# Two groups of heads in one PSUM bank in both attentions of a six-layer decoder kernel on one Trainium2 core

## What is computed

```python
for i in range(NL):
    xn = _adaln(x, noise_emb, n1_w[i], n1_b[i])
    qkv = xn @ qkv_w[i].T
    q, k, v = jnp.split(qkv, 3, axis=-1)
    q = _rope(q.reshape(B, L, H, HD))
    k = _rope(k.reshape(B, L, H, HD))
    v = v.reshape(B, L, H, HD)
    a = _attn(q, k, v, src_mask).reshape(B, L, D) @ so_w[i].T
    x = x + a
    xn = _adaln(x, noise_emb, n2_w[i], n2_b[i])
    q = _rope((xn @ cq_w[i].T).reshape(B, L, H, HD))
    k = _rope((context @ ck_w[i].T).reshape(B, LC, H, HD))
    v = (context @ cv_w[i].T).reshape(B, LC, H, HD)
    a = _attn(q, k, v, ctx_mask).reshape(B, L, D) @ co_w[i].T
    x = x + a
    xn = _adaln(x, noise_emb, n3_w[i], n3_b[i])
    h = jax.nn.gelu(xn @ f1_w[i].T + f1_b[i], approximate=False)
    x = x + (h @ f2_w[i].T + f2_b[i])
```

## Time and profile before

| | us |
|---|---|
| median of 3 runs | 2669.58 (2665.58 to 2670.88) |
| the profiled execution | 2669.4 |
| its span | 2667.6 |
| PE busy in the span | 2461.6 (92%) |
| DVE busy | 2051.6 (77%) |
| ACT busy | 1842.0 (69%) |
| POOL busy | 1079.4 (40%) |

### The profile page before, as it was taken

How to read it: one execution, slowest core, us unless ns; L and a number is a source line. 1 busy time by engine, 2 the same in 40 slices (tenths; PEclk the granted TensorE clock), 3 DMA queues, 4 the chain that set the end, 5 groups by cost and what they waited for, 6 DMA issues and landing times.

```text
span 2667.6 us, 45155 instructions
## 1 busy us (share of the span) xinstructions
PE 2461.6 (92%) x16138; PEld 1064.4 (40%) x16138; DVE 2051.6 (77%) x4303; ACT 1842.0 (69%) x3703; POOL 1079.4 (40%) x1342
## 2 busy tenths in 40 slices
PE   6999899999878899999999999999999999998777
PEld 3445454454512233333333333333333333333444
DVE  6778869778687788888888888888888888875333
ACT  4667666667326677887778877777887777878432
POOL 2545545545533333444344444333443334432311
PEclk9999999999869999999999999999999999999768
DMA  2000000000321121222222222212121212220000
GB/s 75 1 1 1 1 1 1 1 27 1 82 49 42 48 62 48 62 56 73 56 57 64 56 73 59 60 48 71 54 63 50 63 48 56 55 68 22 20 10 8
DMA packets 108569, 113.01 MB, mean 42 GB/s; under 512 B 15809, under 2 KB 96951, under 8 KB 107319
## 3 DMA queue, kind: packets, MB, share of 16 engines
q1 hardware_dynamic: 108345, 110.12, 15.1%
HBM read 14.80 MB, written 1.05 MB: 6 GB/s over the span
## 4 chain that ended last, share of the span: by engine, by line
PE 58%; DVE 22%; POOL 7%; issue 4%; DMA 3%; SPq 3%; ACT 3%; DVEq 0%; POOLq 0%; ACTq 0%
PE psum L1121 8%; DVE A L1591 7%; PE psum L1104 6%; PE psum L917 5%; PE psum L1092 4%; DVE A L1613 4%; PE psum L1027 4%; PE psum L1213 4%; PE psum L1220 3%; PE psum L1002 3%; PE psum L993 3%; SPq L814 2%; DVE nm L1461 2%; PE psum L1185 2%; DMA A<-A 2%
## 5 line engine op out<-in xcount | busy, mean ns | idle before, releaser
L1591 DVE TENSOR_REDUCE A<-psum 128x1 f32<-128x512 f32 x1536 | 1005.4, 684 | 191.8 <-PE psum L1104 178.1
L1808 ACT ACTIVATE A<-psum 128x512 f32<-128x512 f32 x1536 | 821.6, 602 | 149.0 <-PE psum L1121 78.9
L1104 PE MATMUL psum<-A 64*128 64x512 bf16 x1536 | 475.8, 391 | 28.2 <-DVE A L1591 19.5
L1092 PE MATMUL psum<-A 64*128 64x512 bf16 x1536 | 412.4, 386 | 16.5 <-ACT A L1808 8.2
L1121 PE MATMUL psum<-A 128*32 128x512 f32 x3072 | 412.1, 609 | 1.0 <-ACT A L1817 0.2
L1952 POOL TENSOR_TENSOR A<-A,rden 128x512 f32<-128x512 f32 x256 | 264.9, 1056 | 255.0 <-DVE rden L1478 255.0
L1104 PEld LDWEIGHTS psum<-A 64*128 64x128 bf16 x1536 | 120.1, 95 | 454.0 <-DVE A L1591 397.7
L1838 ACT ACTIVATE A<-psum 77x512 f32<-77x512 f32 x384 | 206.6, 592 | 49.2 <-PE psum L1176 47.5
L917 PE MATMUL psum<-ident,A 128*128 128x128 f32 x1264 | 203.6, 288 | 39.9 <-DVE A L1339 13.9
L1983 POOL TENSOR_TENSOR A<-A 128x512 f32<-128x512 f32 (+1 forms) x78 | 96.8, 1241 | 323.2 <-DMA A<-A 319.8
L1749 ACT ACTIVATE A<-psum,nm 128x512 f32<-128x512 f32 x256 | 175.3, 685 | 74.4 <-DVE nm L1464 73.7
(11 more groups left out here) (211 smaller groups left out, 4017.9 us busy)
## 6 DMA issues: line engine op xcount, KB each, us to landing
A<-A SPq DMA_DIRECT2D x456, 128.0 KB, 2.4
A<-A SPq DMA_DIRECT2D x336, 64.0 KB, 2.0
A<-zero SPq DMA_DIRECT2D x51, 128.0 KB, 2.3
wl<-in_wl SPq DMA_DIRECT2D x6, 1024.0 KB, 5.8
A<-A SPq DMA_DIRECT2D x36, 78.0 KB, 2.1
A<-in_nT SPq DMA_DIRECT2D x1, 1664.0 KB, 6.6
A<-in_w SPq DMA_DIRECT2D x2, 512.0 KB, 7.0
A<-in_w SPq DMA_DIRECT2D x1, 1024.0 KB, 5.9
```

The lines of the kernel that those rows point to most:

```text
L1092: handle.matmul(bank(b), k_st[bt][lo:lo + ROW, h // 2, k * P:(k + 1) * P], q_st[m % 3][lo:lo + ROW, h // 2, :], start=True, stop=True).the ...
L1104: handle.matmul(bank(b), q_st[m % 3][lo:lo + ROW, pair, q * P:(q + 1) * P], k_st[bt][lo:lo + ROW, pair, :], start=True, stop=True).then_in ...
L1591: handle.tensor_reduce(nm[:, pair // 4, q, j, pair % 4:pair % 4 + 1], bank(3 + j), AX.X, ALU.max, negate=True).then_inc(mx, 1)
L1808: handle.activation(pT[:, block % 2, i % GROUP, :], bank(ring_of["scores", m, i]), ACT.Exp, scale=HD1 ** -0.5).then_inc(ex, 1)
```

## The change

Groups 2h and 2h+1 form half h. The even group is weighed first, as before with 32 columns, but its slice of the values starts 9 columns earlier, so that its own 9 rows stand at rows 9 to 17 of each strip. The odd group is weighed into the same bank with 9 columns only, and overwrites rows 0 to 8. Then one copy, one turn and one division serve both groups: 2 in place of 4 per step in each attention. The value tiles get 9 unused columns in front. PE waits for the bank before the even group only (`cross_weigh`), ACT for both groups. `divide` takes 32 denominators and 256 results per partition in place of 16 and 128. The columns of the attended matrix come out in another order, so the rows of `so_w` and `co_w` are permuted on the host. All tables have new places; the lengths of `TENSOR`, `SCALAR` and `VECTOR` fall by 4 each (201, 99, 94 to 197, 95, 90); `POOL` keeps its order.

```diff
+HALVES = NG // 2
+HW = HD1 + 1
+V_FIRST = HW
...
+def attended_order():
+    j, half, s, d = np.meshgrid(np.arange(GROUP), np.arange(HALVES), np.arange(2), np.arange(HD1), indexing="ij")
+    return ((GROUP * (2 * half + 1 - s) + j) * HD1 + d).reshape(-1)
...
+        def of_head(t, h, own_rows):
+            lo = V_FIRST + HW * h
+            return t[:, lo:lo + HW] if own_rows else t[:, lo - HW:lo - HW + 32]
...
 TENSOR
-            "o_turn": [246, 319, 356, 403],
+            "o_turn": [700, 785],
-            "co_turn": [656, 658, 674, 692],
+            "co_turn": [1034, 1072],
...
 SYNC
             "layer": -56,
-            "q_swap": -55,
-            "cshift_rows": -12,
-            "q_zero": -53,
+            "q_zero": -55,
+            "q_swap": -54,
+            "cshift_rows": -11,
...
                 if name == "weigh":
...
                     for j in range(GROUP):
-                        lo = (GROUP * g + j) * (HD1 + 1)
-                        t = handle.matmul(psum[32 * j:32 * j + 32, 5, :], v[m % 3][:, k, lo:lo + 32], pT[:, i % 2, j, :],
+                        values = of_head(v[m % 3][:, k, :], GROUP * g + j, g % 2)
+                        t = handle.matmul(psum[32 * j:32 * j + (HW if g % 2 else 32), 5, :], values, pT[:, i % 2, j, :],
                                           start=k == 0, stop=k == QT - 1)
                     t.then_inc(pv_ps, 1)
-                    if k == QT - 1:
-                        owner[5] = (o_sb, 4 * m + g + 1)
+                    if g % 2 and k == QT - 1:
+                        owner[5] = (o_sb, HALVES * m + g // 2 + 1)
                 if name == "o_turn":
-                    pe.wait_ge(o_sb, 4 * m + i + 1)
+                    pe.wait_ge(o_sb, HALVES * m + i + 1)
...
                 if name == "cross_weigh":
-                    free(7)
+                    if i % 2 == 0:
+                        free(7)
...
-            def divide(b, rd_g, att_g):
-                o = bank(b).rearrange("p (q j d) -> p q j d", q=QT, j=GROUP)
-                handle.reciprocal(rd_g, o[:, :, :, HD1]).then_inc(own.next(), 1)
+            def divide(b, half, attended):
+                o = bank(b).rearrange("p (x r) -> p x r", r=32)[:, :, 0:2 * HW].rearrange("p x (s d) -> p x s d", d=HW)
+                handle.reciprocal(rd[:, half, :, :], o[:, :, :, HD1]).then_inc(own.next(), 1)
                 after_own()
...
                 if name == "o_out":
-                    act.wait_ge(pv_ps, 16 * m + 4 * i + 4)
-                    act.wait_ge(ob_ps, 4 * m + i)
+                    act.wait_ge(pv_ps, 16 * m + 8 * i + 8)
+                    act.wait_ge(ob_ps, HALVES * m + i)
```

More of the change, by code:

```diff
@@ new lines, in build @@
+            "qk": [402, 406],
+            "weigh": [574, 583, 602, 607, 618, 648, 673, 681, 695, 696, 710, 718, 738, 749, 755, 765],
+            "cshift_turn": 998,
+            "v": 415,
+            "att_turn": 810,
+            "cross_scores": [1008, 1009, 1013, 1014, 1016, 1019, 1020, 1022, 1025, 1026, 1027, 1035, 1036, 1037, 1055, 1058],
+            "so": 821,
+            "cross_weigh": [1023, 1028, 1061, 1062],
+            "co_turn": [1034, 1072],
+            "ck": [645],
+            "c_turn": 851,
@@ L488, in build @@
+            "x_f": 237,
+            "s_stats": -114,
+            "qk_rope": [-99, -97, -95, -92],
         }
@@ L516, in build @@
         EXPERTS_TENSOR = {
[L517 to L519 removed]
+            ("scores", 40, 23): [("e_turn", 0, 0)],
+            ("cross_max", 0, 22): [("e_logits", 0, 0)],
+            ("f1", 0, 21): [("e_up", 0, 0)],
             ("f2", 0, 21): [("e_up", 1, 0)],
[L521 to L522 removed]
+            ("scores", 63, 23): [("e_up", 2, 0)],
@@ L523, in build @@
+            ("o_turn", 1, 23): [("e_up", 3, 0)],
             ("cshift_turn", 0, 22): [("e_turn2", 0, 0)],
             ("cross_scores", 0, 22): [("e_turn2", 1, 0), ("e_turn2", 2, 0)],
-            ("cross_scores", 3, 22): [("e_turn2", 3, 0)],
+            ("cross_scores", 4, 22): [("e_turn2", 3, 0)],
             ("cross_weigh", 0, 22): [("e_down", 0, 0)],
-            ("cross_weigh", 1, 22): [("e_down", 1, 0)],
-            ("co_turn", 1, 22): [("e_down", 2, 0)],
-            ("c_turn", 0, 23): [("e_down", 3, 0)],
@@ L540, in build @@
-            ("catt_turn", 0, 23): [("e_down", 0, 1)],
-            ("co", 0, 23): [("e_down", 1, 1)],
-            ("f_turn", 0, 23): [("e_down", 2, 1), ("e_down", 3, 1)],
+            ("co_turn", 0, 22): [("e_down", 1, 0)],
+            ("c_turn", 0, 23): [("e_down", 2, 0)],
+            ("cross_scores", 15, 22): [("e_down", 3, 0)],
+            ("f1", 0, 22): [("e_turn", 0, 1)],
+            ("f2", 0, 22): [("e_logits", 0, 1)],
+            ("cross_max", 3, 23): [("e_up", 0, 1)],
+            ("cshift_turn", 0, 23): [("e_up", 1, 1)],
@@ L543, in build @@
+            ("cross_scores", 2, 23): [("e_up", 2, 1)],
+            ("co_turn", 0, 23): [("e_up", 3, 1)],
+            ("cross_weigh", 2, 23): [("e_turn2", 0, 1)],
+            ("co_turn", 1, 23): [("e_turn2", 1, 1)],
+            ("catt_turn", 0, 23): [("e_turn2", 2, 1)],
+            ("co", 0, 23): [("e_turn2", 3, 1)],
+            ("f_turn", 0, 23): [("e_down", 0, 1), ("e_down", 1, 1)],
+            ("f1", 0, 23): [("e_down", 2, 1)],
+            ("f1", 2, 23): [("e_down", 3, 1)],
         }
@@ L1584, in part @@
                 l, bt = divmod(m, B)
-                n = GROUP * HD1
                 if name == "max":
```

217 lines of the change are left out of this document (101 added, 116 removed).

## The result

The changed kernel takes 2653.1 us (median of 4 runs, 2649.8 to 2656.16) against 2670.23 us for the kernel before on the same chip (4 runs, 2665.58 to 2671.61): a ratio of 0.9939, 95% interval 0.9919 to 0.9958. That is 17 us less where 44 were forecast: faster, as foretold, but by 0.6% in place of 1.7%. The profiled execution took 2656.16 us, 13.2 less than that of the kernel before (2669.4); the traces account for this smaller difference.

What follows compares the result with a forecast made beforehand. The prediction took a closed loop over PE, DVE, then SP and POOL to bound the kernel: 1.38 + 0.45 = 1.83 us per pass, times 24 steps, 44 us off 2669.4, giving 2625 us. The range was 2578 to 2656, the forecast's own 2597 to 2655.

Steps and rivals of the forecast that it cites:

- The closed loop: One steady pass, 70.09 us, is a loop over PE, DVE, then SP and POOL; savings count only where they lie in it.
- DVE stretch: From `x_f` to `qk_rope`, 16.94 us: one maximum fewer (0.60), a larger division (+0.15), so 0.45 us shorter.
- POOL stretch: SP and POOL from the rope through swap and `c_norm` to the next `c_turn`: stays at 18.44 us.
- Two leave the PE stretch: 2 x 0.69 = 1.38 us: PE stretch, `c_turn` to `x_f`, 34.71 us: two of four dropped turns lie there, saving 1.38 us per pass.
- And the bf16 matmuls are 65 in both: nothing: Between `c_turn` and `f2`, the old and new orders hold equally many bf16 matmuls: no change in time.
- One `weigh` leaves and one `cross_weigh` enters, nothing: Between `c_turn` and `f2` on PE, the two weighings exchanged cost 1.00 us each: no change.
- I count all 24: The saving of 1.83 us per pass applies to all 24 steps, filling and end included: 44 us.
- Divisions: On DVE, enlarged reciprocal 270 ns and product 425 ns; one division lies in the loop, +0.15 us per pass.
- Nine columns: Every second weighing on PE, 32 columns cut to 9: no change from 1.00 us, at best 0.15 less.
- 1, PE alone counts: All four turns and new pairing count on PE: 4.1 us per pass, 98 us, total 2571; chance 0.2.
- 3, nine rows not side by side: Nine-row matmuls on PE stop sharing the array: 3.4 us more per group, total 3441 us; chance 0.06.
- 2, the order gives it back: New places bring an equal wait, for instance for cross exponentials: about 1.8 us per pass, total 2669; chance 0.12.

Runs made afterwards that it cites:

- a1: Changed kernel with the first cross turn of each step issued twice, between `f2` and `c_turn`: 2655.17 us (kernel before 2670.05), regular pass 69.3.
- a3: Changed kernel with one more POOL instruction of 1.04 us in `c_norm`: 2693.01 us (kernel before 2670.05), regular pass 70.2 to 70.3.
- b1: Changed kernel with one more POOL instruction of 1.04 us in `f_norm`: 2667.64 us (kernel before 2670.05), regular pass 69.3 to 69.4.
- a4: Changed kernel with one DVE maximum per step ahead of the ropes computed twice: 2667.97 us (kernel before 2665.68), regular pass 69.9.
- c1: Changed kernel with `cross_weigh` 2, between `c_turn` and `f1`, cut from 512 to 64 columns: 2659.51 us (kernel before 2667.52), regular pass 69.3.
- i1: Changed kernel with maxima 5 to 8 over 256 of 512 keys and `cross_weigh` 2 cut to 64 columns: 2649.79 us (kernel before 2660.69), regular pass 68.9.
- c3: Kernel before with `o_turn` 1 and 2 cut from four pieces to one: 2666.68 us (uncut 2667.52), regular pass 69.7 to 69.9.
- i2: Changed kernel with maxima 5 to 8 over 256 of 512 keys: 2647.67 us (kernel before 2660.69), regular pass 69.2.
- c2: Changed kernel with `cross_weigh` 0, between `f2` and `c_turn`, cut from 512 to 64 columns: 2653.8 us (kernel before 2667.52), regular pass 69.3.

## Why the prediction was wrong, step by step

- **The closed loop, and its cut into three stretches**: right (a1, a3, b1, a4). DVE stretch: forecast -0.45, measured 16.94 to 16.41 (`x_f` 1815.80, rope 1832.21). POOL stretch: forecast 0, measured 18.44 to 18.42.
- **"Two leave the PE stretch: 2 x 0.69 = 1.38 us"**: this step failed. The stretch went from 34.71 to 34.50. The size of a turn was not far off: in the PE stretch two turns fewer hold PE 1.15 us less by distance between starts, 0.58 each. What failed is that this time leaves the stretch. PE is busiest there, but PE alone isn't what the time is made of. From `c_turn` to `maximum` 8 PE and DVE run in chains of nearly the same length, and what leaves PE alone comes back as waits: 0.75 us cut in the changed kernel gave 0.0 (c1) and counted only together with DVE's maxima (i1, 0.43). In the kernel before, `o_turn` 1 cut by three pieces gave 0.0 (c3), so a turn there had no price in the old order either. Between `f1` and `f2` it has one: the shorter `o_turn` 2 gave 0.33 for three pieces. But of the whole turn that the change takes away there only 0.18 was found, as four bf16 matmuls now stand ahead of `f2` in place of one.
- **"And the bf16 matmuls are 65 in both: nothing"**: by distance between starts, from `c_turn` to `x_f`, the 65 with their waits hold PE 11.03 us before and 12.27 after, 1.24 more; turns hold it 1.15 less (28 pieces of turning, now 20), weighings 0.20 and cross maxima 0.10 less. The sum is the 0.2 that was found. It is the same failure seen from the other side. By the written order two half-array matmuls that can run side by side need one slot: that makes 36 slots before and 35 after. But in the trace of these two stretches 25 pairs start together before (under 0.01 us apart) and only 20 after. The others start one behind the other, most likely because one of them waits for its bank.
- **"One `weigh` leaves and one `cross_weigh` enters, nothing"**: right in its sum. That it is forced by bank 7 I hadn't seen.
- **"I count all 24"**: failed. 19 passes gained 18.0 us, the filling lost 2.6 and the end gained 0. A filling isn't a bare chain that each saved turn shortens: from the first value projection to the first `f2` it took 263.1 us in the changed kernel (260.5 before), 261.8 with four maxima shortened (i2, 707.8 to 969.6), 268.5 with 1.04 us more in `f_norm` (b1, 714.0 to 982.5). It was no shorter than before in any run of the new order, and its granted clock was lower (0.81, it was 0.84). Which of the new places brings that wasn't tried and stays open.
- **Divisions**: the product was right (424 ns, forecast 425), the reciprocal 0.08 us too cheap; one division is in the loop, so that is 0.08 us a pass.
- **Nine columns**: right. A group of nine starts 0.98 us ahead of what follows it (1857.02 to 1858.00), where 1.00 stood. By the Trainium skill (TensorE: Matmul & The Clock Gate, LDWEIGHTS) a load takes its columns over 1.2 GHz; the estimate from it was that eight exposed loads would have saved 0.15 us. The row shows 0.02, so hardly any of that time was exposed.
- **Rivals.** 1, PE alone counts: ruled out by a1, c1 and c2. 3, nine rows not side by side: ruled out by the same 0.98. 2, the order gives it back, came nearest in what happened: the gain of the PE stretch was given back through waits, though the wait that I named, for cross exponentials ahead of the two adjacent cross weighings, isn't in the trace (they run from 1854.51 to 1856.37 without one; it shows only in c1 and i1, 0.23 us, when the first is cut short), and the DVE stretch kept its own.

So the regular pass gained 0.56 us in the covered part, 0.18 from `f1` to `f2` and 0.02 between, 0.76 in all, where the forecast had 1.83. Nineteen times 0.76 is 14.4 of the 18.0 us; the rest came in the longer passes, which I didn't take apart. The total of 2653.1 us lies just inside the range of the forecast (2597 to 2655), whose upper end stood for 0.6 us a pass. That is no support for the mechanism: the DVE stretch gave what was forecast (0.53 us, forecast 0.45), and the PE stretch, which was to give three times as much, gave 0.21.

## What to carry to other kernels

A closed loop found in a trace says where added time counts, and not that removed time counts there: where two engines' chains of the same length run side by side (as can happen in an order that was fitted by hand), test a removal on each chain and on both before putting a price on it. An engine that is busy 97% may still be paced by its partners, when short waits lie between its short instructions. And a new buffer layout and the order around it are one change: this layout in the old order was 68 us slower in one run, in its own 17 us faster.
